# Feed-forward of a decoder layer by seven block products per pair of row tiles

## The chip, the cores and the metric

One core of a Trainium2 chip runs the whole kernel. The metric is the time of one execution in device microseconds, the median of several runs.

## The reference

The input x has 16 batches of 256 rows of 2048 numbers, 4096 rows in all. A layer does three things, each followed by a residual sum and a layer norm:

```python
x = _layernorm(x + _L0_attn_ref(x))              # autocorrelation along the row
x = _layernorm(x + _L0_xattn_ref(ctx, ctx, x))   # attention of 256 rows over 256 context rows
x = _layernorm(x + _L0_ffn_ref(x, W_base, gate_W, A, B))
# the last one, on rows xf of 2048 numbers:
gate_probs = softmax(xf @ gate_W.T)              # 8 experts
weights, sel = top_k(gate_probs, 2); weights = weights / sum(weights)
h = einsum('td,erd->ter', xf, A) * (w_dense[:, :, None] * 2.0)   # 8 experts x rank 8
out = xf @ W_base.T + einsum('ter,eor->to', h, B)                # W_base is 2048 x 2048
```

The change concerns the third of them, the feed-forward: a product with a 2048 x 2048 matrix, a router that picks two of eight experts for each row, and a LoRA term from a stack of 64 numbers per row.

## The kernel before, in words

`decoder_layer` runs `setup`, `attention_pass` (the first two things of the layer, on 16 batches), reads a verdict flag, and runs a slow exact autocorrelation only if a row needs it; with these inputs none does. Then `feed_forward` follows. `attention_pass` leaves its result x2 in HBM (`x_scratch` in the profile). At its end its SP queue already loads what the feed-forward starts with: the first 128 rows (`xn0`), the router and A matrices (`ag_raw`), and three chunks of W_base.

`feed_forward` works on 32 tiles of 128 rows. Every f32 operand is split in a high and a low f16 part, and a product is three matmuls: high x high, high x low of the weights, low of the rows x high. For a tile, `main(j)` runs 16 steps of 128 in the contraction x 3 terms for each of four blocks of 512 columns, in PSUM bank `ps_y[j]` (line 1143): 192 matmuls. `experts` computes the router scores and the A part in 16 pairs of narrow matmuls (lines 1162 and 1163) with 144 and 72 columns. `transposed_h` (line 1170) turns the weighted h by two TensorE transposes, and `lora(j)` adds two matmuls to each bank (lines 1147, 1148). The weights are loaded once as 32 chunks of two steps x 512 columns, scaled and split (ScalarE line 938 the high part, VectorE line 1012 the low one, and every fourth from the eighth on by GpSimd in lines 920 and 921). They stay in SBUF.

The row operands: SP loads a tile of x2 (`load`, line 875), ScalarE writes the high half of all 2048 numbers (line 949), VectorE the low one (line 1029), and SP issues two DMA transposes (lines 896 and 898) to `x_hi` and `x_lo`, double-buffered by tile; the first two tiles are turned by TensorE instead (line 1128). A bank is emptied by `bank_out(j)` on VectorE (line 1023): PSUM x inverse scale + the residual row, into `y`. Then come statistics (line 1039) and aggregation (line 1111) on VectorE, four small operations on GpSimd (lines 926 to 929), normalising on ScalarE (line 999) and the store by SP (line 901). TensorE waits in `main(j)` only until bank j of the tile before is empty. TensorE, VectorE, ScalarE and GpSimd run this over the middle tiles in a loop of two tiles a turn. Each engine executes its list in the written order, and semaphores tie the lists.

## Time and profile before

| | us |
|---|---|
| median of 3 runs | 2074.72 (2074.20 to 2074.81) |
| the profiled execution | 2074.21 |
| its span, first to last instruction | 2072.4 |

The profile is one execution. Its page has the busy time of each engine (PE is TensorE's matmuls, PEld its weight loads, DVE is VectorE, ACT ScalarE, POOL GpSimd, SP the queue that issues the DMAs), the chain of work that ended last, and groups of instructions by line. The attention fills roughly the first 590 us and the feed-forward the rest. A matmul's busy time is longer than the distance to the next one, since matmuls are pipelined: for what one costs, read the distance between starts. PEclk is the clock granted to TensorE as a share of 2.4 GHz; 0.50 is 1.2 GHz. The DMA share is the mean busy share of the core's 16 DMA engines.

### The profile page before, as it was taken

The page shows a single profiled execution, that of the slowest core. Times are in us where ns is not written, and L with a number is a line of the kernel's source. Part 1 is how long each engine was busy: PE and PEld are TensorE (multiplying, and loading weights), DVE is VectorE, ACT ScalarE, POOL GpSimd, SP SyncE. Part 2 cuts the span into 40 slices and gives each one's busy share as a digit, 9 for nine tenths or more (in the row PEclk, how much of TensorE's full clock was granted, in tenths as well). Part 3 has the DMA queues.
Part 4 walks back from the last instruction along what each step waited for, and adds up shares of the span by engine and source line. Part 5 has one row for each costly group of instructions (what it writes and reads, how often), then busy time and mean ns, then how long its engine had stood idle before and what let it go on. Part 6 is the DMA issues. An engine that isn't in the chain of part 4 may idle for free.

```text
span 2072.4 us, 28247 instructions
## 1 busy us (share of the span) xinstructions
PE 1952.7 (94%) x11266; PEld 1046.0 (50%) x11266; DVE 855.5 (41%) x2169; ACT 607.0 (29%) x771; POOL 318.3 (15%) x527
## 2 busy tenths in 40 slices
PE   3898989898957999999999999999999999999998
PEld 3666666666623444444444444444444444444443
DVE  4777777787757332222232222232222223222221
ACT  5777777778546110000010000010000011000000
POOL 3344444444315000000000000000000000000000
PEclk9999999999979999999999999999999999999999
DMA  8899999999667232121232111222111122211121
GB/s 265 231 281 260 291 269 282 266 288 272 203 211 249 85 93 66 61 61 61 71 100 71 61 61 61 61 97 85 61 61 61 61 81 92 70 61 61 61 61 41
DMA packets 288910, 271.17 MB, mean 131 GB/s; under 512 B 261504, under 2 KB 261632, under 8 KB 265984
## 3 DMA queue, kind: packets, MB, share of 16 engines
q1 hardware_dynamic: 288832, 270.17, 43.6%
q8 instruction: 44, 0.72, 0.1%
q14 instruction: 34, 0.28, 0.0%
HBM read 138.02 MB, written 67.11 MB: 99 GB/s over the span
## 4 chain that ended last, share of the span: by engine, by line
PE 67%; ACT 1%; DVE 1%; DMA 1%; issue 1%; POOL 1%; ACTq 0%; POOLq 0%
PE ps_y_f L1143 62%; PE ps_a_f L1162 2%; PE ps_y_f L1147 1%; PE ps_y_f L1148 1%; PE ps_a_f L1163 1%; ACT w_hi_f L938 1%; DMA cbuf<-w_chunks 0%; DVE w_lo_f L1012 0%; DMA chunk<-w_chunks 0%; POOL w_lo_f L921 0%; POOL cbuf L920 0%; PE ps_h_f L1170 0%; DVE b_stack_f L1098 0%; ACT y_f L999 0%; PE ps_t_f L1128 0%
## 5 line engine op out<-in xcount | busy, mean ns | idle before, releaser
L1143 PE MATMUL ps_y_f<-w_hi_f,x_hi_f 128*128 128x512 f16 x2048 | 777.5, 380 | 11.8 <-POOL w_lo_f L921 8.1
L1143 PE MATMUL ps_y_f<-w_lo_f,x_hi_f 128*128 128x512 f16 x2048 | 777.4, 380 | 0.0
L1143 PE MATMUL ps_y_f<-w_hi_f,x_lo_f 128*128 128x512 f16 x2048 | 777.2, 379 | 0.0
L999 ACT ACTIVATE y_f<-y_f,nb_f,rs_f 128x2048 f32<-128x2048 f32 x32 | 67.0, 2093 | 1112.3 <-POOL nb_f L929 1112.3
L1143 PEld LDWEIGHTS ps_y_f<-w_hi_f,x_hi_f 128*128 128x128 f16 x2048 | 200.6, 98 | 249.5 <-POOL w_lo_f L921 10.5
L1143 PEld LDWEIGHTS ps_y_f<-w_hi_f,x_lo_f 128*128 128x128 f16 x2048 | 200.7, 98 | 242.5 <-issue 1.4
L1143 PEld LDWEIGHTS ps_y_f<-w_lo_f,x_hi_f 128*128 128x128 f16 x2048 | 200.7, 98 | 233.5 <-issue 1.1
L1023 DVE SCALAR_TENSOR_TENSOR y_f<-ps_y_f,w_iscale,xn_f 128x512 f32<-128x512 f32 x64 | 46.6, 749 | 476.5 <-PE ps_y_f L1148 476.5
L1023 DVE SCALAR_TENSOR_TENSOR y_f<-ps_y_f,w_iscale,xn 128x512 f32<-128x512 f32 x64 | 46.6, 748 | 448.4 <-PE ps_y_f L1148 448.4
L926 POOL TENSOR_TENSOR var_eps_f<-mv_f,columns 128x1 f32<-128x1 f32 x32 | 6.1, 190 | 1357.1 <-DVE mv_f L1111 1357.1
L675 PE MATMUL ps_s_fast<-k_both_fast,q_hi_fast 128*128 128x256 f16 x1024 | 170.1, 274 | 6.2 <-DMA k_both_fast<-v_lo_fast 5.3
L675 PE MATMUL ps_s_fast<-k_both_fast,q_lo_fast 128*128 128x256 f16 x512 | 140.3, 274 | 0.0
L534 DVE SCALAR_TENSOR_TENSOR x2buf_fast<-ps_c_fast,iscale_fast,xbuf_fast 128x512 f32<-128x512 f32 x128 | 96.0, 750 | 70.3 <-PE ps_c_fast L664 69.5
L675 PEld LDWEIGHTS ps_s_fast<-k_both_fast,q_hi_fast 128*128 128x128 f16 x1024 | 100.6, 98 | 21.7 <-DMA k_both_fast<-v_lo_fast 5.5
L505 DVE TENSOR_TENSOR q_lo_fast<-ps_t_fast,q_hi_fast 128x512 f16<-128x512 f32 x128 | 86.2, 685 | 48.1 <-ACT q_hi_fast L389 48.0
L664 PE MATMUL ps_c_fast<-v_hi_fast,p_hi_fast 128*128 128x512 f16 x256 | 97.0, 379 | 0.1
L664 PE MATMUL ps_c_fast<-v_hi_fast,p_lo_fast 128*128 128x512 f16 x256 | 97.0, 379 | 0.0
L664 PE MATMUL ps_c_fast<-v_lo_fast,p_hi_fast 128*128 128x512 f16 x256 | 97.0, 379 | 0.0
L646 PE MATMUL ps_t_fast<-ident,xbuf_fast 128*128 128x128 f32 x512 | 75.0, 281 | 14.4 <-ACT xbuf_fast L422 9.0
L1039 DVE BATCH_NORM_STATS2 stats_f<-y_f 128x6 f32<-128x512 f32 x128 | 85.3, 687 | 2.2
L714 PE MATMUL ps_t_fast<-ag_raw,fwd_fast 128*128 128x256 bf16 x512 | 61.1, 273 | 25.9 <-ACT power_fast L465 25.9
L646 PEld LDWEIGHTS ps_t_fast<-ident,xbuf_fast 128*128 128x128 f32 x512 | 62.2, 145 | 37.6 <-DVE q_lo_fast L505 12.9
(161 smaller groups left out, 2081.4 us busy)
## 6 DMA issues: line engine op xcount, KB each, us to landing
xbuf_fast<-x SPq DMA_DIRECT2D x32, 1024.0 KB, 7.7
x_scratch<-x2buf_fast SPq DMA_DIRECT2D x32, 1024.0 KB, 6.0
out<-y_f SPq DMA_DIRECT2D x32, 1024.0 KB, 4.0
cbuf<-ctx_in SPq DMA_DIRECT2D x16, 1024.0 KB, 5.7
cbuf_fast<-ctx_in SPq DMA_DIRECT2D x16, 1024.0 KB, 6.8
xn<-w_chunks SPq DMA_DIRECT2D x16, 1024.0 KB, 7.6
xn<-x_scratch SPq DMA_DIRECT2D x16, 1024.0 KB, 4.8
xn_f<-x_scratch SPq DMA_DIRECT2D x16, 1024.0 KB, 4.8
```

Of the source, the lines that this page charges most:

```text
L505: v.tensor_tensor(q_lo[at], bank, q_hi[at], ALU.subtract).then_inc(t_free, 1)
L534: v.scalar_tensor_tensor(x2buf[parity][:, r, b * BANK:(b + 1) * BANK], ps_c[j % 2][:], iscale[parity][:], xbuf[parity][:, r, b * BANK:(b + ...
L646: ins = nc.tensor.transpose(bank[:, i * P:(i + 1) * P], xbuf[other][:, r, (kk + i) * P:(kk + i + 1) * P], ident[:])
L664: ins = nc.tensor.matmul(ps_c[j % 2][:], pp[:, d, r * P:(r + 1) * P], vv[parity][:, d, b * BANK:(b + 1) * BANK], start=(i == 0), stop=(i = ...
L675: ins = nc.tensor.matmul(ps_s[r][:, 0:C], qq[:, k, r * P:(r + 1) * P], k_both[other][:, k, part, :], start=(i == 0), stop=(i == 3 * KT - 1))
L714: ins = nc.tensor.matmul(ps_t[m % 3][:, 0:C], fwd[:, k, m * P:(m + 1) * P], u_t[:, k, :], start=(k == 0), stop=(k == HALF // P - 1))
L938: nc.scalar.activation(w_hi[chunk_at(c)], chunk[buffer_of[c]], ACT.Copy, scale=w_scale[:]).then_inc(w_hi_done, 1)
L999: nc.scalar.activation(y[parity][:], y[parity][:], ACT.Identity, bias=nb_[:, 0:1], scale=rs[:, 0:1]).then_inc(out_ready, 1)
L1023: v.scalar_tensor_tensor(y[parity][:, at], ps_y[j][:], w_iscale[:], xn[parity][:, at], ALU.mult, ALU.add).then_inc(evacuated, 1)
L1039: return v.bn_stats(stats[:, j], y[parity][:, j * BANK:(j + 1) * BANK])
L1143: nc.tensor.matmul(ps_y[j][:], xx[parity][:, k], ww[:, k, j * BANK:(j + 1) * BANK], start=(k == 0 and xx is x_hi and ww is w_hi), stop=False)
L1162: nc.tensor.matmul(ps_a[:, 0:2 * AG], x_hi[parity][:, k], ag_t[:, k, :], start=(k == 0), stop=False)
```

## The change

The feed-forward is rewritten; of the attention only the prefetch at its end changes (one load of 1 MB for the first weight unit in place of three of 0.5 MB). No arithmetic of the attention changes.

Rows are taken in 16 pairs of tiles, and output columns in two passes of 1024. For a pair and a pass, the operand rows are a 2 x 2 grid of blocks of 128 rows x 1024 numbers (A11, A12 the first tile's halves, A21, A22 the second's), the weights a 2 x 2 grid of 1024 x 512, and the output a 2 x 2 grid of 128 x 512. The four output blocks are built from seven products of sums of blocks in place of eight products. There are 32 slots: 0 to 15 are the pairs in order for the first 1024 columns, 16 to 31 the pairs in reverse order for the others; slot 16 uses the operands of slot 15 again. The lists of all engines are written out, without loops.

- The seven row operands of a slot: two plain blocks and five sums (`combine`, VectorE, 128 x 1024 f32), each split in a high half (`high_rows`, ScalarE) and a low half (`low_rows`, VectorE) and turned by one DMA transpose of 128 x 2048 f16 (`turn`, SP). `rows` has two buffers, `a_cols` one place per product. Operand i of slot s + 1 is turned when product i of slot s is done.
- The seven weight operands: for each of eight steps of a pass, `unit_low` makes five sums and differences in four VectorE instructions (1024, 512, 512 and 512 columns) and three low parts (1024, 1536 and 1024), `unit_high` three high parts on ScalarE. GpSimd takes no part. The second pass's weights overwrite the first's during slots 15 and 16.
- The seven products use seven PSUM banks. `update` adds a bank, times plus or minus the inverse scale, to a block of y: 14 updates of 128 x 512 a slot. y begins as the residual, loaded by SP from x2.
- The first pass's y goes to HBM (`y_scratch`) and comes back in the second pass for the statistics and the norm. The h of the router goes through `h_scratch`.
- The router of a pair works on both tiles at once (`router_scores`, `router_weights`), its scores run a pair ahead from slot 1 on, as narrow matmuls on four of the seven operands. Slots 0, 15 and 16 (`sweeps`) have the step as the outer loop over all seven products; the others finish one product after the other.

The core of the diff:

```diff
-                for c in range(PREFETCHED):
-                    sp.dma_start(consts["chunks"][c].rearrange("p k c -> p (k c)"), chunk_rows(w_chunks, c)).then_inc(prefetched, 16)
+                sp.dma_start(consts["cbuf0"][:], w_chunks[0]).then_inc(prefetched, 16)
...
+    OPERANDS = [(A22,), (A11,), (A21, A11, ALU.subtract), (A21, A22, ALU.add), (A12, A22, ALU.subtract), (A11, A22, ALU.add),
+                (A11, A12, ALU.add)]
+    W_SLOT = [1, 0, 2, 5, 3, 4, 6]
+    SCORED = (0, 1, 2, 4)
+    PRODUCT = {0: [(0, C11, 1), (0, C21, 1)], 1: [(1, C12, 1), (1, C22, 1)], 3: [(3, C21, 1), (3, C22, -1)],
+               5: [(5, C11, 1), (5, C22, 1)], 6: [(6, C12, 1), (6, C11, -1)], "L12": [("L12", C12, 1)],
+               "L21": [("L21", C21, 1)], "L22": [("L22", C22, 1)], "L11": [("L11", C11, 1)]}
...
+                def next_block(s, b):
+
+                    if s > 1 and makes(s) and s != NP_ + 1:
+                        if b in (A11, A12):
+                            sp.wait_ge(a_sum, 5 * made(s))
+                        else:
+                            sp.wait_ge(a_lo, item(s, 0) - NM + (4 if b == A21 else 6))
+                        load_block(s, b)
+
+                def turn(s, i):
+
+                    if makes(s):
+                        g = item(s, i)
+                        sp.wait_ge(a_lo, g + 1)
+                        if s:
+                            sp.wait_ge(pe_done, ev(s - 1, "S1" if s - 1 == 1 and i in SCORED else i))
+                        sp.dma_start_transpose(a_cols[:, i], rows[g % 2][:].rearrange("p a c -> p (a c)")).then_inc(a_turned[g % 2], 16)
...
+                    if s == NP_:
+                        sp.wait_ge(w_lo_done, 3 * (2 * HK - 1))
+                        for b in (A22, A21):
+                            load_block(s + 1, b)
+                        sp.wait_ge(w_lo_done, 3 * 2 * HK)
+                        for b in (A11, A12):
+                            load_block(s + 1, b)
+                        load_first(s)
+                    turn(s + 1, 0)
+                    turn(s + 1, 1)
+                    if s > NP_:
+                        store_out(s - 1)
+                    turn(s + 1, 2)
+                    if s > NP_:
+                        load_first(s)
+                    turn(s + 1, 3)
+                    next_block(s + 2, A21)
+                    load_residual(s + 1)
+                    turn(s + 1, 4)
+                    if s < LAST:
+                        store_h(s)
+                    turn(s + 1, 5)
+                    for b in (A22, A11, A12):
+                        next_block(s + 2, b)
+                    load_h(s + 1)
+                    turn(s + 1, 6)
...
+                    v.tensor_tensor(both[:, 0:2], raw[:, 0::2], raw[:, 1::2], ALU.add).then_inc(w_sum, 1)
+                    v.tensor_tensor(both[:, 2], raw[:, 0], raw[:, 3], ALU.add).then_inc(w_sum, 1)
+                    dve.wait_ge(w_sum, 4 * u + 1)
+                    v.tensor_tensor(raw[:, 1], raw[:, 1], raw[:, 3], ALU.subtract).then_inc(w_sum, 1)
+                    v.tensor_tensor(raw[:, 2], raw[:, 2], raw[:, 0], ALU.subtract).then_inc(w_sum, 1)
+                    low(slice(5, 7), raw[:, 0::3], 1)
+                    low(slice(2, 5), both, 2)
+                    low(slice(0, 2), raw[:, 1:3], 3)
...
+                def update(s, *which):
+
+                    for u in which:
+                        origin, (t, j), sign = updates(s)[u]
+                        acc = y[s % 2][:, t, j * BANK:(j + 1) * BANK]
+                        so_far = [w for w in range(u) if updates(s)[w][1] == (t, j)]
+                        if so_far:
+                            dve.wait_ge(added, NU * s + so_far[-1] + 1)
+                        else:
+                            dve.wait_ge(residual, 16 * (s + 1))
+                        dve.wait_ge(pe_done, ev(s, origin))
+                        v.scalar_tensor_tensor(acc, bank[bank_of(s, origin)][:], (w_iscale if sign > 0 else minus_iscale)[:], acc, ALU.mult,
+                                               ALU.add).then_inc(added, 1)
...
+                    low_rows(s + 1, 0)
+                    if 1 < s < LAST:
+                        router_scores(s)
+                    combine(s + 1, 2)
+                    low_rows(s + 1, 1)
+                    if 1 < s < LAST:
+                        router_weights(s)
+                    update(s, 0, 1)
+                    low_rows(s + 1, 2)
+                    combine(s + 1, 3)
+                    update(s, 2, 3)
+                    combine(s + 1, 4)
+                    low_rows(s + 1, 3)
+                    update(s, 4, 5)
+                    low_rows(s + 1, 4)
+                    combine(s + 1, 5)
+                    if late(s):
+                        router_scores(s)
+                    else:
+                        update(s, 6, 7, 8, 9)
+                    combine(s + 1, 6)
+                    low_rows(s + 1, 5)
+                    if late(s):
+                        router_weights(s)
+                        update(s, 6, 7)
+                    else:
+                        update(s, 10, 11)
+                    low_rows(s + 1, 6)
+                    if late(s):
+                        update(s, 8, 9)
+                    if s > NP_:
+                        block_stats(s, C21)
+                        block_stats(s, C22)
+                        first_stats(s)
...
+                def step(i, kk):
+
+                    for part, ww in ((0, w_hi), (0, w_lo), (HK, w_hi)):
+                        ins = nc.tensor.matmul(bank[i][:], a_cols[:, i, part + kk, :], ww[:, W_SLOT[i], kk, :],
+                                               start=(kk == 0 and part == 0 and ww is w_hi), stop=(kk == HK - 1 and part == HK and i not in (2, 4)))
+                    return ins
+
+                def product(s, i):
+
+                    wait_slot(s, i)
+                    wait_bank(s, i)
+                    for kk in range(HK):
+                        ins = step(i, kk)
+                    done(ins, s, i)
...
+                def sweep(s):
+
+                    for kk in range(HK):
+                        if s != LAST:
+                            pe.wait_ge(w_lo_done, 3 * (HK * (s // NP_) + kk + 1))
+                        for i in range(NM):
+                            if kk == 0:
+                                wait_slot(s, i)
+                                wait_bank(s, i)
+                            ins = step(i, kk)
+                            if kk == HK - 1:
+                                done(ins, s, i)
+                                if i == 2:
+                                    lora(s, "L22")
+                                if i == 4:
+                                    lora(s, "L11")
...
```

## Rows read from the trace of the kernel before

**Rows 1.** Page, part 1: busy us (share of the span) and instructions.

```profile
PE 1952.7 (94%) x11266; PEld 1046.0 (50%) x11266; DVE 855.5 (41%) x2169; ACT 607.0 (29%) x771; POOL 318.3 (15%) x527
```

**Rows 2.** Page, part 4: the chain that ended last, by engine.

```profile
PE 67%; ACT 1%; DVE 1%; DMA 1%; issue 1%; POOL 1%; ACTq 0%; POOLq 0%
```

**Rows 3.** Windows: the attention, steady tiles; first line names the columns.

```profile
core 0: us, PE busy (x) PEld busy (x) DVE busy (x) ACT busy (x) POOL busy (x), PEclk, DMA share, GB/s
0.00:560.00 560.00, 483.20 (x3568) 345.52 (x3569) 415.28 (x959) 406.86 (x579) 247.60 (x370) 0.99 0.93 267
1000.00:1500.00 500.00, 500.00 (x2609) 236.51 (x2608) 130.67 (x385) 50.45 (x45) 11.84 (x44) 1.00 0.23 70
```

**Rows 4.** Timeline of SP: start, duration us, line; first transposes of two tiles.

```profile
1040.06 1.52 SPq L896 DMA_TRANSPOSE x_hi_f<-cbuf  x1
...
1084.95 1.67 SPq L896 DMA_TRANSPOSE x_hi_f<-cbuf  x1
```

**Rows 5.** Chain in order of time, from 590 us: start, us, what.

```profile
686.06 10.36 PE ps_y_f L1143 x48
```

**Rows 6.** Timeline, router scores in a steady tile.

```profile
1077.15 0.20 PE L1163 MATMUL ps_a_f<-ag_t_f,x_lo_f 128*128 128x72 f16 x1
...
1077.24 0.20 PE L1163 MATMUL ps_a_f<-ag_t_f,x_lo_f 128*128 128x72 f16 x1
```

**Rows 7.** Timeline, where the feed-forward begins, ScalarE and TensorE.

```profile
599.24 1.06 ACT L966 ACTIVATE y_f<-ag_raw 128x1024 f32<-128x1024 f32 x1 [9.48 <-issue]
...
612.25 0.63 PE L1143 MATMUL ps_y_f<-w_hi_f,x_lo_f 128*128 128x512 f16 x1
612.67 0.63 PE L1143 MATMUL ps_y_f<-w_hi_f,x_hi_f 128*128 128x512 f16 x1
```

**Rows 8.** Windows of the start, columns as in Rows 3.

```profile
613.00:615.00 2.00, 2.00 (x6) 0.76 (x5) 2.00 (x2) 2.00 (x4) 0.00 (x0) 0.50 0.39 96
617.00:619.00 2.00, 2.00 (x10) 0.87 (x9) 2.00 (x2) 2.00 (x3) 0.00 (x0) 0.94 0.77 227
639.00:641.00 2.00, 0.34 (x2) 0.00 (x0) 2.00 (x2) 0.05 (x1) 2.00 (x1) 1.00 0.97 406
```

**Rows 9.** Groups of VectorE by shape: busy us, mean ns, idle before.

```profile
L505 DVE TENSOR_TENSOR q_lo_fast<-ps_t_fast,q_hi_fast 128x512 f16<-128x512 f32 x128 | 86.2, 685 | 48.1 <-ACT q_hi_fast L389 48.0
...
L1029 DVE TENSOR_TENSOR cbuf<-xn,cbuf 128x2048 f16<-128x2048 f32 x15 | 34.3, 2285 | 0.2 <-ACT cbuf L949 0.2
...
L1079 DVE TENSOR_SCALAR dense_f<-expert_ids,top_f_f,wtop_f 128x8 f32<-128x8 f32 x32 | 9.3, 291 | 1.2
```

**Rows 10.** Timeline of VectorE: two weight low parts, two bank updates, two statistics.

```profile
615.56 2.48 DVE L1012 SCALAR_TENSOR_TENSOR w_lo_f<-y_f,w_scale,w_hi_f 128x1024 f16<-128x1024 f32 x2
...
1055.27 1.41 DVE L1023 SCALAR_TENSOR_TENSOR y_f<-ps_y_f,w_iscale,xn_f 128x512 f32<-128x512 f32 x2 [11.90 <-PE ps_y_f L1148]
1056.60 1.28 DVE L1039 BATCH_NORM_STATS2 stats_f<-y_f 128x6 f32<-128x512 f32 x2
```

**Rows 11.** Groups of ScalarE by shape.

```profile
L999 ACT ACTIVATE y_f<-y_f,nb_f,rs_f 128x2048 f32<-128x2048 f32 x32 | 67.0, 2093 | 1112.3 <-POOL nb_f L929 1112.3
...
L938 ACT ACTIVATE w_hi_f<-cbuf,w_scale 128x1024 f16<-128x1024 f32 x12 | 13.6, 1144 | 7.6 <-DMA cbuf<-w_chunks 7.5
```

**Rows 12.** Page, part 6: DMA issues, median us to landing.

```profile
x_hi_f<-cbuf SPq DMA_TRANSPOSE x30, 3.8
```

**Rows 13.** The attention's transposes to k_both, issued by SP.

```profile
DMA to landing us min/median/max: 4.2/4.8/12.6
```

**Rows 14.** Windows: two transposes alone, plain loads; columns as in Rows 3.

```profile
1041.00:1047.00 6.00, 6.00 (x31) 2.78 (x30) 2.37 (x2) 0.39 (x1) 0.00 (x0) 1.00 0.77 175
631.00:633.00 2.00, 2.00 (x11) 0.89 (x10) 1.74 (x12) 1.22 (x2) 0.00 (x0) 1.00 1.03 422
```

**Rows 15.** Timeline of the end: last matmul and last store.

```profile
2062.43 0.38 PE L1148 MATMUL ps_y_f<-b_stack_f,ag_raw 128*128 128x512 f16 x1
...
2068.09 0.33 SPq L901 DMA_DIRECT2D out<-y_f  x1
```

951 lines of the change are left out of this document (582 added, 369 removed).

## The prediction

> **What bounds the kernel now.** I read the totals first, then the chain, then stages. TensorE is busy 94% of the span, VectorE 41%, ScalarE 29% [rows 1], and 67% of the chain that ended last is TensorE [rows 2]. The windows say where: between 1000 and 1500 us TensorE is busy all 500 us at full clock, while VectorE has 131 us, ScalarE 50 and the DMA engines a share of 0.23 [rows 3]. So in the feed-forward only TensorE's own instructions count. From one row transpose to that of the next tile are 44.89 us [rows 4]. 48 main matmuls take 10.36 us, 0.216 each [rows 5]; a pair of router matmuls takes 0.095 [rows 6]. 200 wide ones (192 main, 8 LoRA) make 43.2 us, 16 router pairs 1.5, two transposes 0.1: 44.8, the tile. The sum closes, no wait is hidden in it. The block begins its work at 599.2 and its first matmuls run 0.42 us apart [rows 7]. The attention before it is only touched in its prefetch.
>
> **The change, part by part.** *Matmuls.* A pair of tiles now takes 384 main matmuls. With seven products of two halves it takes 2 passes x 7 products x 8 steps x 3 terms = 336. LoRA stays at 16 a pair. Router matmuls stay too: four operands x 8 steps x a hi/lo pair = 32 pairs against 2 x 16. A first-pass slot (pair of tiles, half of the columns) is 176 x 0.216 = 38.0, plus 32 x 0.095 = 3.0, plus four transposes 0.2: 41.2 us. A second-pass slot is 38.0. Together 79.2 against 89.8, so 10.6 less a pair and 169 us over 16 pairs, if TensorE stays the bound.
>
> *VectorE.* No row adds two f32 tensors in SBUF. The nearest are subtractions: 2048 columns 2.28 us, 512 columns 0.69 [rows 9]. That is 1.04 ns a column, so 1024 columns are 1.2 us, and some 1.14 from start to start, because successive starts lie about 0.08 closer than the durations (two of 1.28 each end within 2.48 [rows 10]). The bounds are half of that, were such an addition to run at double rate, and 1.2. I take 1.14. A slot has 5 sums and 7 low halves (12 x 1.14 = 13.7) and 14 bank updates of 0.66 (two in 1.41 [rows 10]) = 9.2. The router of two tiles is some 29 small operations, none over 0.29 [rows 9]; I take 6, at most 8.4. That makes 29 of 41.2 us in the first pass. In the second, eight statistics at 0.6 [rows 10] and the aggregation replace the router: 28.5 of 38.0. VectorE is in order and waits in between for TensorE, but each product's operand is made a slot ahead and a bank is reused six products later, so a lag under some 10 us reaches nobody.
>
> *ScalarE.* 7 high halves of 1.1 [rows 11], and in the second pass four normalising halves of about 1.05: 12 of 38 us. Hidden.
>
> *Transposes.* 217 of them in place of 60, all from SP, each with 2 KB a partition as before. One lands after 3.8 us [rows 12], next to the attention's traffic typically 4.8 and at most 12.6 [rows 13]. Two row buffers alternate, so two items take one round: landing 3.8, high half 1.1, low half 1.2, handovers: some 7 us, 25 a slot. SP also waits for product i before it overwrites operand i. Queued behind that wait are the block loads of a later pair, the residual and the stores; each has between 5 and 30 us until it is needed.
>
> *DMA engines.* Two transposes alone held a share of 0.77 over 6 us, 2.3 us each; a plain stream ran at 422 GB/s [rows 14], so 1 MB is 2.5 us. A second-pass slot moves 7 transposes (16.2 us) and 6.3 million bytes (2 MB of x, 1 residual, 1 of first-half result in, 2 out: 15 us) = 31 of 38. But in the attention the mix got 267 GB/s at a share of 0.93 [rows 3]; at that price the 10 million bytes of such a slot take 35 us. The first-pass slot moves 4.3 plus 3.7 million: 26 to 28 of 41. I count both as hidden. Without the cover see the first rival.
>
> *The start.* TensorE now needs all seven operands for its first step, and VectorE makes the weight sums. One unit (1/8 of a half): one 1024-wide sum 1.14, three of 512 at 0.61, low parts 1.20 + 1.75 + 1.20: 7.1 us, against 21 x 0.216 = 4.5 of TensorE. From 599.2, VectorE's list (four units, seven low halves, five sums, scale steps) ends at 643; the seventh transpose lands by 648. Until then TensorE idles for the most part at half clock; two cold steps cost 3 us more (before, the clock rose about 6 us after the first matmuls [rows 7, 8]). Router scores are done at 664, and VectorE, waiting for them, goes on with units 6 and 7 and the weights until 685. The last step ends at 690. The next slot waits for the bank that only the last updates free (13 x 0.66 and five other operations after 685): 698. It has two pairs' scores: 45.4, to 743. Thirteen slots of 41.2: 1279.
>
> *The turn of the passes.* Slots 15 and 16 walk the steps outermost while eight new units are made. VectorE: end of the last slot and router 7, bias stack 1, eight units 57, 15 updates 10, hence the last unit at 79 after the turn; TensorE ends 4.5 + 1 later, 84.5. Slot 17's operands come after that: blocks of x wait for the stage buffer, then 2 MB go ahead of the first transpose, so products 0 to 2 run late by 4 us. VectorE's backlog (13 updates, 12 sums and halves) delays slot 18's first bank by 5. I get 169 us for slots 15 to 18 where 152 would be undisturbed: 1448. Thirteen more of 38.0: 1942.
>
> *The end.* Before, from the last matmul to the end were 10.0 us [rows 15]. Now two updates, two statistics and four shorter ScalarE operations with two stores follow: 13.5. Sum: 1955. The profiled execution took 2074.2 with a span of 2072.4; with those 1.8 us around it the forecast is 1957. The median of the runs, 2074.7, is 0.5 above it.
>
> **A rule on the clock.** Between two steps of the paced slots TensorE would wait 2.6 us. In the old start it was busy 0.34 of 2 us at 639 and still had the full clock [rows 8]. The Trainium skill (TensorE: Matmul & The Clock Gate, HAM oscillation) says that a step shorter than its wait falls back to the low clock each time. By the trace the sum above stands; by that rule ten steps take 9 us in place of VectorE's 7.1.
>
> **Rivals.** *DMA binds the second pass.* For: at the attention's rate the slot needs 35 of 38 us, and SP issues in order with waits between, so the engines can't be filled. Against: each 1 MB has about 5 us of spread, and 422 GB/s was reached. Were a slot 40.5 to 43, 15 slots add 38 to 75: 1995 to 2032.
>
> *VectorE's order binds.* Its 75% are counted without semaphore times; 2 us a slot over 29 slots: 2015; 1 us: 1986. Against: the slack of 10 us at each bank.
>
> *The low clock in the paced steps.* By the rows of cold matmuls, 0.42 apart [rows 7], a step of 21 takes 9 us; ten steps 19 us more: 1976. Against it stands the window at 639.
>
> *Slower than before: the transpose round.* If transposes in the new, denser traffic land late, the two row buffers set the slot: 7 items x (landing + 2.9)/2. From a landing of about 8 us this exceeds a second-pass slot; from about 9.5 us, 43.4 a slot, the gain of all is gone, and at the longest landing seen, 12.6 [rows 13], a slot is 54 us and the kernel takes about 2370. For: 3.6 times the transposes and more plain bytes beside them. Against: typical landings in the attention at a share of 0.93 were 4.8.
>
> *It doesn't do what it says.* All streams are now written out; if TensorE's longer stream ran short of instructions, each of 5400 matmuls at 0.25 instead of 0.216 would eat the gain. Against: the attention, written out too, kept TensorE busy 483 of 560 us with shorter instructions [rows 3].
>
> **How the numbers follow.** Forecast as worked: 0.62, 1942 to 1972 (VectorE's additions at double rate would give some 25 us back at start and turn; small waits add). DMA-bound second pass 0.17. VectorE's order 0.09. Low clock 0.05. Transposes' round 0.04, split between little gain and a loss. Not as said 0.03. The forecast is 1957. The range of 8 in 10 takes in the forecast's, the clock's, most of VectorE's and a good half of the DMA's case: 1938 to 2020. A measurement here can tell about 0.2%, 4 us, from no change. Faster 0.94, same 0.01, slower 0.05.
>
> **What would show it.** Right: main matmuls 5376; in 800 to 1200 and 1500 to 1900 us TensorE busy throughout, VectorE at 0.70 to 0.75; slots 41.2 and 38.0 apart; first full step at about 650; slot 1 starting near 698; steps 7.1 apart near 1330 to 1360 with the clock at 1.00. Wrong: TensorE waiting for transposes in the second pass with landings over 6 us and a DMA share near 0.9 (first rival), waits for updates on VectorE in mid-slot (second), 0.50 in the clock column at the turn (third).

## The result, and the profile after

| | before | after |
|---|---|---|
| median, us | 2074.76 (4 runs, 2074.20 to 2078.83) | 2016.6 (4 runs, 2013.05 to 2023.17) |
| the profiled execution | 2074.21 | 2013.05 |
| its span | 2072.4 | 2011.1 |

The ratio of the times is 0.9719, with a 95% interval of 0.9691 to 0.9747. The kernel is 58 us faster; the forecast was a gain of 118 us. The direction was right and 2016.6 lies in the range, near its end, but the gain is only half of what the forecast 1957 promised.

Page of the changed kernel, part 1 (busy us, share of the span, instructions) and the lines of part 2 that show the stages:

```profile
PE 1801.7 (90%) x10466; PEld 968.3 (48%) x10466; DVE 1459.2 (73%) x2673; ACT 799.4 (40%) x984; POOL 308.7 (15%) x449
...
PE   3899989999862879999999999997799999999997
...
PEclk9999999999985989999999999999899999999998
DMA  8899999999859497888888787736999999999994
```

TensorE's busy time fell by about the work removed, its share from 94% to 90% [rows 1]. VectorE went from 41% to 73%. In the last line the DMA engines, at 0.23 in the middle of the old feed-forward [rows 3], are at 7 or 8 tenths in the first pass and at 9 in the second until its last slice.

A slot is read from the start of its first main matmul (line 1486) to that of the next slot. The terms of the forecast stand against these lengths, in us of the profiled execution:

| stretch | forecast | measured | miss |
|---|---|---|---|
| start, until slot 1 begins | 698 | 698.6 | +0.6 |
| slot 1 | 45.4 | 63.8 | +18.4 |
| slots 2 to 14 | 13 x 41.2 | 13 x 41.25 | +0.7 |
| slots 15 to 18 | 169 | 38.3 + 51.1 + 56.1 + 38.0 = 183.5 | +14.5 |
| slots 19 to 31 | 13 x 38.0 = 494 | 514.6, 39.6 each on average (38.0 to 43.9) | +20.6 |
| end | 13.5 | 14.4 | +0.9 |

The misses add to 55.7; 2011.1 - 1955 is 56.1, and the difference is rounding. Three places hold 53.5 of it. Windows of the steady parts (columns as in [rows 3]): slots 4 to 14, slots 19 to 31, and slots 19 to 30 alone, since in slot 31 no further operands are made:

```profile
845.50:1298.60 453.10, 453.10 (x2681) 224.98 (x2680) 320.84 (x660) 90.92 (x110) 0.00 (x0) 1.00 0.81 192
1482.10:1996.70 514.60, 498.89 (x2289) 223.54 (x2287) 362.71 (x479) 148.54 (x137) 45.64 (x52) 0.99 0.98 247
1482.10:1958.60 476.50, 460.79 (x2114) 206.45 (x2113) 339.95 (x444) 142.09 (x132) 44.41 (x48) 0.99 1.01 254
```

In the first pass TensorE has no gap at all (453.10 of 453.10), VectorE 0.71. In the second, TensorE stands 15.7 of 514.6 us. Slots 19 to 30 are 39.7 us each, and the DMA share in them is 1.01 where I had counted "31 of 38" to "35 of 38". The waits of the same stretch (engine, line, what it waited for: us in all, times, longest):

```profile
ACT rows_f L1114 <- DMA a_cols_f<-rows_f: 242.0, 48, 8.3
DVE rows_f L1233 <- ACT rows_f L1114: 140.4, 47, 6.8
...
PE bank_f L1524 <- DVE y_f L1272: 15.7, 10, 4.3
```

Read from below: TensorE's LoRA matmuls (line 1524) wait for an update of VectorE (line 1272), and VectorE, in order, stands before that update at a low half (line 1233) whose high half is not there. In all, ScalarE is late with high halves mostly because a row buffer is still read by a transpose (242.0 us), but right before TensorE's waits there is one link more. The longest of them ends at 1593.4. VectorE and ScalarE before it:

```profile
1571.91 1.23 DVE L1233 TENSOR_TENSOR rows_f<-sums_f,rows_f 128x1024 f16<-128x1024 f32 x1 [6.79 <-ACT rows_f L1114]
...
1589.63 1.23 DVE L1233 TENSOR_TENSOR rows_f<-sums_f,rows_f 128x1024 f16<-128x1024 f32 x1 [5.15 <-ACT rows_f L1114]
```

```profile
1570.82 1.06 ACT L1114 ACTIVATE rows_f<-sums_f 128x1024 f16<-128x1024 f32 x1 [8.34 <-DMA a_cols_f<-rows_f]
...
1584.02 1.24 ACT L1154 ACTIVATE cbuf<-cbuf,nb_f,rs_f 128x1024 f32<-128x1024 f32 x1 [2.11 <-POOL nb_f L1096]
...
1588.56 1.04 ACT L1114 ACTIVATE rows_f<-sums_f 128x1024 f16<-128x1024 f32 x1
```

A late transpose holds ScalarE for 8.34 us and VectorE behind it for 6.79. Its statistics come late by that, then GpSimd's four operations, then ScalarE's four normalising halves (lines 1154 and 1155). They stand in ScalarE's list ahead of the high half that VectorE needs at 1589.6. The same normalising halves stand before each of the seven waits of over 1 us in slots 19 to 30. So the name at TensorE is VectorE's, the far end of the chain is a DMA, and between them lies the order of ScalarE's list. The transposes themselves (SP's instruction in ns, then landing), first pass and second:

```profile
L947 SPq DMA_TRANSPOSE a_cols_f<-rows_f x77: 1317/1960/4992, 844.4 to 1292.2; - x77
...
DMA to landing us min/median/max: 4.2/4.6/7.4
```

```profile
L947 SPq DMA_TRANSPOSE a_cols_f<-rows_f x87: 1317/3398/7962, 1479.8 to 1968.2; - x87
...
DMA to landing us min/median/max: 4.2/6.0/10.2
```

A landing of 3.8 [rows 12] was assumed. No transpose here lands in under 4.2, and the median of the second pass is 6.0. Slot 1 has a wait of another kind (waits from 699 to 765):

```profile
PE bank_f L1515 <- DVE ag_raw L1339: 13.5, 1, 13.5
PE bank_f L1486 <- DVE y_f L1272: 6.9, 1, 6.9
PE bank_f L1524 <- ACT ag_raw L1148: 1.5, 1, 1.5
```

The 6.9 end at 698.6 and belong to the forecast's start (its "698"). The 13.5 are new: the transposed h of slot 1 waits for the last operation of the router on VectorE, and 1.5 more for ScalarE's copy of it. After each of the two long waits TensorE runs at the low clock: 0.50 from 698 to 702 and again from 746 to 758.

### The profile page after: what moved, and what is told of

It reads as the page before. It is cut to its first block and busy times, and to the rows that moved or that the text cites. A ratio compares the mean times of both kernels' runs of the same rounds, so it can differ in the third digit from the quotient of the medians.

```text
span 2011.1 us, 27872 instructions
## 1 busy us (share of the span) xinstructions
PE 1801.7 (90%) x10466; PEld 968.3 (48%) x10466; DVE 1459.2 (73%) x2673; ACT 799.4 (40%) x984; POOL 308.7 (15%) x449
## 5 line engine op out<-in xcount | busy, mean ns | idle before, releaser
L1486 PE MATMUL bank_f<-w_hi_f,a_cols_f 128*128 128x512 f16 x3584 | 1093.1, 382 | 75.8 <-DMA a_cols_f<-rows_f 60.0
L1486 PE MATMUL bank_f<-w_lo_f,a_cols_f 128*128 128x512 f16 x1792 | 685.4, 382 | 0.0
L1486 PEld LDWEIGHTS bank_f<-w_hi_f,a_cols_f 128*128 128x128 f16 x3584 | 353.1, 99 | 506.8 <-DVE w_lo_f L1241 41.8
L1272 DVE SCALAR_TENSOR_TENSOR y_f<-bank_f,w_iscale,y_f 128x512 f32<-128x512 f32 x384 | 269.4, 743 | 137.2 <-PE bank_f L1486 98.0
L1486 PEld LDWEIGHTS bank_f<-w_lo_f,a_cols_f 128*128 128x128 f16 x1792 | 176.4, 98 | 205.5 <-issue 5.2
L1114 ACT ACTIVATE rows_f<-xn_f 128x1024 f16<-128x1024 f32 x93 | 98.2, 1056 | 380.1 <-DMA xn_f<-x_scratch 152.0
L1233 DVE TENSOR_TENSOR rows_f<-sums_f,rows_f 128x1024 f16<-128x1024 f32 x93 | 113.6, 1221 | 166.5 <-ACT rows_f L1114 166.3
L1114 ACT ACTIVATE rows_f<-sums_f 128x1024 f16<-128x1024 f32 x93 | 97.9, 1052 | 324.7 <-DMA a_cols_f<-rows_f 317.2
L1233 DVE TENSOR_TENSOR rows_f<-xn_f,rows_f 128x1024 f16<-128x1024 f32 x93 | 112.7, 1212 | 24.7 <-ACT rows_f L1114 24.4
L339 POOL TENSOR_TENSOR u_rows_fast<-xbuf_fast 128x1024 bf16<-128x1024 f32 x32 | 75.7, 2366 | 33.4 <-DMA xbuf_fast<-x 26.8
```

The source lines that it names most:

```text
L339: g.tensor_tensor(u_rows[:, r], xbuf[parity][:, r, 0:HALF], xbuf[parity][:, r, HALF:L], ALU.subtract).then_inc(folded, 1)
L1114: nc.scalar.activation(rows[g % 2][:, 0], source(i), ACT.Copy).then_inc(a_hi, 1)
L1233: v.tensor_tensor(rows[g % 2][:, 1], source(i), rows[g % 2][:, 0], ALU.subtract).then_inc(a_lo, 1)
L1272: v.scalar_tensor_tensor(acc, bank[bank_of(s, origin)][:], (w_iscale if sign > 0 else minus_iscale)[:], acc, ALU.mult, ALU.add).then_inc(a ...
L1486: ins = nc.tensor.matmul(bank[i][:], a_cols[:, i, part + kk, :], ww[:, W_SLOT[i], kk, :], start=(kk == 0 and part == 0 and ww is w_hi), st ...
```

## The experiments

Four questions: what makes a slot of the second pass 39.6 us and not 38.0; what makes slot 1 63.8 and not 45.4; what the turn of the passes loses; and whether the answers give a faster kernel. Slot lengths are those of one execution each. The changed kernel itself spreads over 10 us between executions, so whole times serve here only for differences beyond that, the lengths of slots for the rest. As a measure of what slot lengths mean: with the second pass unchanged, slots 19 to 30 average 39.7 us in the changed kernel, 39.9 with the scores ahead in slot 1, and 40.0 with stores added in the first pass.

### Slot 1: the scores before the products

In the changed kernel slot 1 gives its event `S1` only after the scores of operand 4, which stand behind five products, and the transposes of slot 2 wait for that event. The forecast had not seen this wait. The edit puts each operand's scores ahead of its product, so that a transpose waits for its own product only:

```diff
-            return [0, 1, 2, 3, 4, "S1", 5, 6, "L22", "L11", "L12", "L21", "S2"]
+            return [0, 1, 2, 3, "S1", 4, 5, 6, "L22", "L11", "L12", "L21", "S2"]
-                            sp.wait_ge(pe_done, ev(s - 1, "S1" if s - 1 == 1 and i in SCORED else i))
+                            sp.wait_ge(pe_done, ev(s - 1, i))
...
-                        product(s, i)
-                        if late(s):
-                            if i in SCORED:
-                                ins = scores(s, i)
+                        if late(s) and i in SCORED:
+                            ins = scores(s, i)
                             if i == 4:
                                 done(ins, s, "S1")
-                        else:
+                        product(s, i)
+                        if not late(s):
```

> Slot 1 takes 63.8 us in the changed kernel, 18 more than counted. In slot 1 the transposes of operands 0, 1, 2 and 4 of slot 2 wait until all router scores of slot 1 are done, 31 us into the slot; VectorE reaches the router of slot 1 only behind the low half of operand 5. Here each operand's scores are computed before its product, and a transpose waits for its own product alone. Theory (the wait for the scores holds the row work back and with it the router): slot 1 falls to 46 to 50 us, TensorE's wait before the transposes of h (13.5 us) goes to under 2, the kernel gets 14 to 18 us faster. Rival (the transposes' own round of issue, landing, high and low half sets the slot, whatever releases it): slot 1 stays above 56 us. The slots from 2 on stay as they are.

Measured: 2008.35 us; slot 1 58.6 in place of 63.8. The event cost 5.2 us, not 14 to 18, and 58.6 lies where the rival put it. What is left (waits from 697 to 760):

```profile
PE bank_f L1515 <- DVE ag_raw L1339: 10.8, 1, 10.8
PE bank_f L1524 <- ACT ag_raw L1148: 0.7, 1, 0.7
```

### The second pass: order on SP, bytes, or VectorE

Three edits. The first moves the stores, the load of the first half, the residual and three of four x blocks to GpSimd's queue from slot 17 on. The second loads 128 of the 1024 columns of each first half, 0.9 MB less a slot:

```diff
-                    sp.dma_start(y_first, y_scratch[token(s)]).then_inc(first_loaded, 16)
+                    sp.dma_start(y_first[:, :, 0:P], y_scratch[token(s)][:, :, 0:P]).then_inc(first_loaded, 16)
```

The third leaves out VectorE's four statistics of the first half from slot 17 on.

> From slot 17 on the stores of the result, the loads of the first half, of the residual and of three of the four blocks of x are issued by GpSimd instead of SP; the bytes are the same, and A21 and h stay on SP. Second-pass slots 19 to 31 take 39.6 us on average in the changed kernel against 38.0 of TensorE's work. Theory A (order: in one queue a transpose stands behind 1 to 2 MB of plain transfers, lands after 6 to 9 us in place of 4.3, and the row work and VectorE's updates get late): slots 38.0 to 38.4, transposes land in 4 to 5.5 us. Theory B (capacity: the DMA engines at a share of 0.98 can carry no more): slots stay at 39.2 or more whichever queue issues. Theory C (VectorE's own time): no change either.

> The load of the first half's result in the second pass brings 128 of 1024 columns per row tile; the rest of that half of the output is computed from old contents of the buffer. That is 0.9 million bytes less of 10 in each second-pass slot, with all other work kept. Theories A (order) and B (capacity) both say that slots 19 to 31 fall from 39.6 to 38.0 to 38.6 us; by B the DMA share stays near 0.95. Theory C (VectorE's own time) says 39.6 as before.

> The four statistics instructions on the first half are left out from slot 17 on, so the norm there uses old statistics; VectorE has 2.45 us less in each second-pass slot, all DMAs stay. Theory C (VectorE's own time binds the second pass): slots 19 to 31 fall from 39.6 to 38.0 to 38.3 us. Theories A and B: VectorE stands idle for ScalarE's halves anyway, slots fall by at most 0.6 us.

Measured: 2076.21, 1994.42 and 2025.66 us. Without 0.9 MB every slot from 18 to 30 is 37.99 us and TensorE has no wait left, although transposes still land after a median of 5.1 us and up to 10.2. Without the statistics (2.5 us less for VectorE a slot) slots 19 to 30 average 40.7, no better than 39.7; TensorE waited 23.5 us for updates. So bytes count, and less work for VectorE gained nothing. With the plain transfers on GpSimd's queue slots 19 to 30 rose to 44.5. That one left two readings: an expensive issuer, or a second queue of any kind. Windows of slots 19 to 30 with 0.9 MB less, and of the second pass with GpSimd's queue:

```profile
1484.00:1939.90 455.90, 455.90 (x2114) 206.67 (x2113) 343.38 (x449) 143.91 (x133) 44.52 (x48) 1.00 0.98 244
```

```profile
1490.00:2016.00 526.00, 470.51 (x2093) 206.84 (x2092) 334.05 (x437) 139.38 (x131) 67.72 (x132) 0.96 1.00 227
```

At a share of 0.98 of 37.99 us, 37.2 us of the engines, nothing waits; at 1.01 it does.

### Added stores in the first pass

```diff
+                def spill_out(s, n):
+                    if 3 <= s <= 13 and n < (2 if s <= 8 else 4):
+                        sp.dma_start(spill[spills[0]], consts["cbuf0"][:]).then_inc(spilled, 16)
+                        spills[0] += 1
...
+                    spill_out(s, 1)
                     turn(s + 1, 3)
...
                     turn(s + 1, 4)
+                    spill_out(s, 0)
...
+                    spill_out(s, 2)
                     turn(s + 1, 6)
+                    spill_out(s, 3)
```

> The second pass of the changed kernel moves some 10 MB a slot (2 MB more than the first) at a DMA share of 0.99 and takes 39.6 us a slot where TensorE needs 38.0; leaving 0.9 MB out gave 38.0. Two theories are left. Capacity: the engines are simply full, at (0.99 x 39.6 - 0.79 x 41.25) / 2 = 3.3 us for each further MB. Order: what counts is that transposes stand behind plain transfers on SP's queue and land at 6 to 10 us instead of 4.3, however full the engines are. This kernel adds stores of 1 MB each from an idle buffer to a spare DRAM area in the first pass: two in each of slots 3 to 8 (10 MB a slot, as in the second pass), four in each of slots 9 to 13 (12 MB). Capacity: slots 3 to 8 need 32.6 + 6.6 = 39.2 us of the engines, under TensorE's 41.25, and stay at 41.25 each without a wait of TensorE; slots 9 to 13 need 32.6 + 13.2 = 45.8 and take 45 to 47 at a share of 0.99 or more; the kernel takes about 2040. Order: already slots 3 to 8 show landings of 6 to 10 us, waits of TensorE and 42 to 44 us a slot.

Measured: 2027.06 us. Windows of slots 3 to 8, 9 to 11 and 12 to 14:

```profile
804.30:1051.80 247.50, 247.50 (x1469) 122.91 (x1466) 175.28 (x361) 49.59 (x60) 0.00 (x0) 1.00 0.95 246
1051.80:1175.50 123.70, 123.70 (x735) 61.37 (x732) 85.75 (x179) 24.80 (x30) 0.00 (x0) 1.00 0.99 266
1175.50:1308.10 132.60, 124.81 (x737) 60.99 (x735) 87.19 (x181) 24.91 (x31) 0.00 (x0) 1.00 1.00 263
```

With the bytes of a second-pass slot, slots 3 to 8 are 41.25 us each and TensorE never waits; the engines are busy 0.95 x 41.25 = 39.2 us of them, as expected to the tenth. Transposes land there after a median of 4.8 us and 8.2 at most, where the theory of order wanted 6 to 10. Two stores cost (0.95 - 0.81) x 41.25 = 5.8, so 2.9 us for each MB. Four stores were expected to bind at once; in fact slots 9 to 11 still took 41.25, and only 12 to 14 stretched to 45.2, 43.8 and 43.6. In slots 9 to 11 the engines moved 266 GB/s, 11.0 million bytes a slot of the 12.1 asked for, so the rest fell behind into the slots after. The theory of order falls as the main cause: 10 MB with plain transfers at similar places of SP's list do no harm where the slot is 41.25, and cost 1.6 to 1.7 where it is 38.0. The engines' capacity decides, at 39.2 us for this mix; the 0.5 us from there to 39.7 no run explains.

### Plain copies for the transposes

```diff
-                        sp.dma_start_transpose(a_cols[:, i], rows[g % 2][:].rearrange("p a c -> p (a c)")).then_inc(a_turned[g % 2], 16)
+                        sp.dma_start(a_cols[:, i].rearrange("p k c -> p (k c)"), rows[g % 2][:].rearrange("p a c -> p (a c)")).then_inc(a_turned[g % 2], 16)
```

> Every transpose of the feed-forward is replaced by a plain copy of the same 0.5 MB between the same two buffers, so the columns of x are not transposed and all main products, the router's scores and the whole output are other values; the number of instructions and of waits stays. If the transposes are what fills the engines (7 of them at some 2.9 us, 20 of 39 us, against 1.3 for plain data at the 2.5 us a MB of an undisturbed stream, 9 us), the DMA share of the first pass falls from 0.79 to about 0.5 and that of the second from 0.99 to about 0.7, landings are 3 us or less, all slots of the second pass take 38.0, slot 17 falls below 50, and the kernel takes 1975 to 1990. If copies within SBUF cost the engines as much as transposes, the shares stay and so do the 39.6 us.

Measured: 1986.51 us. First and second pass:

```profile
850.00:1290.00 440.00, 440.00 (x2608) 218.61 (x2607) 309.90 (x634) 88.73 (x106) 0.00 (x0) 1.00 0.51 190
1490.00:1950.00 460.00, 460.00 (x2133) 208.49 (x2131) 340.71 (x446) 145.60 (x134) 45.74 (x50) 1.00 0.72 266
```

The bytes are the same, the share falls from 0.81 to 0.51 and from 1.01 to 0.72, and all slots from 18 on are 37.99. Per transpose that is (0.81 - 0.51) x 41.25 / 7 = 1.8 us more than a plain copy in the first pass, and (1.01 x 39.7 - 0.72 x 38.0) / 7 = 1.8 in the second. The whole second-pass slot of 10 MB takes 0.72 x 38.0 = 27.4 us when all of it is plain, 2.7 us a MB, so a plain 0.5 MB is about 1.4 and a transpose some 3.2. The packet records of the changed kernel give 2.9 to 3.0 directly: the transposes' packets of 256 bytes take 20.6 us of the engines in a first-pass slot and 20.9 in a second-pass one. The Trainium skill (Advanced Engine Details and Errata, X-Bar Transpose (TRN2)) states that "TRN2 transpose DMAs are as fast as regular DMAs"; by these runs, for 0.5 MB within SBUF, one takes more than twice as long. Slot 17 stayed at 53.2 and slot 1 at 60.9, each 2.9 us shorter: neither is mainly a matter of what a transpose costs.

### Orders alone: router of slot 1, updates of the second pass

```diff
+                    if s > NP_:
+                        update(s, 0, 1)
                     low_rows(s + 1, 1)
...
+                    if late(s):
+                        router_scores(s)
+                    if s > NP_:
+                        update(s, 2, 3)
                     low_rows(s + 1, 2)
                     combine(s + 1, 3)
+                    if late(s):
+                        router_weights(s)
```

(ScalarE's exponential and its copy of h move ahead accordingly; the scores stand ahead of the products, as above.)

> Orders alone. (1) Slot 1, on top of scores before products: VectorE's router scores and weights of slot 1 stand right behind the event of the scores (in place of after the sum of operand 5 and the low half of operand 5), ScalarE's exponential and the copy of h stand ahead of the high halves 2 and 5. In the run with the scores ahead alone, TensorE still waited 10.8 us for the router's last operation and 0.7 for the copy; if that is all that is left, slot 1 falls from 58.6 to 46 to 48 us. If the transposes bind slot 1 instead, it stays over 54. (2) Second pass: the updates of product 0 and of product 1 stand ahead of the low halves 1 and 2 of the next slot. TensorE waits 15.7 us in all there for updates that the LoRA products need, each time with VectorE held by a low half that waits for a late transpose. If VectorE's order turns late transposes into TensorE's waits, these waits go and the slots fall from 39.6 to 38.0 to 38.3. If the DMA engines' capacity binds, the waits only move to the transposes (TensorE waiting for a_cols) and the mean stays at 39.3 to 39.9. Whole: 1980 to 1985 with the first, about 1997 with the second.

Measured: 2029.94 us. Both halves went against the wish. Slot 1 is 61.2 although the router's wait is gone; other waits stand in its place (from 702 to 765, without the one that ends where slot 1 begins):

```profile
PE bank_f L1510 <- DMA a_cols_f<-rows_f: 6.6, 1, 6.6
PE bank_f L1491 <- DVE y_f L1270: 4.2, 1, 4.2
PE bank_f L1529 <- ACT ag_raw L1148: 2.7, 1, 2.7
```

In the second pass the LoRA matmuls no longer wait, and the slots rise to 40.9: TensorE now waits 27.5 us, 11 times, at a slot's first product for the bank that the last updates of the slot before free. My reading, not tested by itself: VectorE standing at an update that TensorE has not made ready delays the next operand, which keeps a row buffer longer. At a full share (1.00 in slots 19 to 30) this order moved the wait and lost about 1 us a slot. An order that moves ScalarE's normalising halves behind the high halves that VectorE needs, the link seen in the profile above, was not run.

### Stores and one load on ScalarE's queue

> The two stores of the result and the load of the first half move from SP's queue to ScalarE's in the second pass (3 MB of the 6.5 MB of plain data), with the same bytes; in the earlier run with plain transfers on GpSimd's queue the slots rose to 44. If SP's order is the limit (plain transfers ahead of transposes in one ring), transposes land in 4.3 to 6 us more often and the second pass falls to 38.0 to 38.5 a slot, the kernel to 1995 to 2000. If the engines' capacity is the limit, the slots stay at 39.3 to 40 and the kernel at 2008 to 2017; if a second queue mixes its packets between those of a transpose and slows it, they rise above 40.5.

Measured: 2070.15 us, the third case: slots 19 to 30 average 43.8. Window of slots 19 to 30 and, below it, the transposes of the second pass:

```profile
1490.40:2016.00 525.60, 473.80 (x2112) 209.17 (x2113) 340.11 (x445) 143.46 (x133) 40.27 (x48) 0.95 1.02 231
```

```profile
L947 SPq DMA_TRANSPOSE a_cols_f<-rows_f x85: 1667/3527/14579, 1488.4 to 2014.1; - x85
...
DMA to landing us min/median/max: 4.2/7.2/19.8
```

At a full share the engines move 231 GB/s in place of 254, and a transpose lands after up to 19.8 us. GpSimd's queue had given 227. So it is not the one issuer that costs: plain data from a second queue beside transposes makes them dearer. By the packet records the transposes of a slot take 24.3 us of the engines in both runs where they took 20.9, and the plain data 19.6 and 19.2 where it took 18.6. The Trainium skill (DMA: Bandwidth & Descriptors, Rules for kernel authors) states that spreading DMAs over queues doesn't help, since all run on the same 16 engines. By these two runs it does harm: 4.1 and 4.8 us a slot.

### Three operands kept from the first pass

The first pass has room (0.81 of 41.25 us), the second has none, and a transpose costs more than twice what a plain transfer of its size does. So, with the scores ahead in slot 1 as well, operands 4, 5 and 6, once transposed, go to HBM in slots 1 to 14 and come back as plain loads in slots 17 to 30:

```diff
+                def keep(s, i):
+                    if 0 < s < LAST and i in KEPT:
+                        g = item(s, i)
+                        sp.wait_ge(a_turned[g % 2], 16 * (g // 2 + 1))
+                        sp.dma_start(a_scratch[s, KEPT.index(i)], a_cols[:, i].rearrange("p k c -> p (k c)")).then_inc(a_kept, 16)
...
+                    if kept(s, i):
+                        g = item(s, i)
+                        sp.wait_ge(a_lo, g + 1)
+                        sp.wait_ge(pe_done, ev(s - 1, i))
+                        sp.dma_start(a_cols[:, i].rearrange("p k c -> p (k c)"), a_scratch[token(s), KEPT.index(i)]
+                                     ).then_inc(a_turned[g % 2], 16)
+                        return
```

> The runs so far say: the second pass is bound by the DMA engines (10 MB a slot, 39.2 us of them); a transpose of 0.5 MB costs 3.0 us of them where a plain copy of the same size costs 1.3; the first pass has 8 us a slot to spare. This kernel (with the scores ahead in slot 1) uses that: operands 4, 5 and 6, transposed in the first pass, are stored to a DRAM area (slots 1 to 14) and loaded from there in the second pass (slots 17 to 30) where they were summed, split and transposed again; a placeholder of one column keeps the counts. Same result. First pass: 1.5 MB more, 32.6 + 5 = 37.6 us of the engines, so 41.25 a slot. Second pass: 3 x (3.0 - 1.6) = 4.1 us less, 35.1 us: slots 19 to 30 at 38.0 each, share near 0.92. VectorE also loses 3 sums and 3 low halves, 7 us a slot, which lets slots 17 and 18 end 3 to 8 us earlier. Whole 1980 to 1988. Rival (latency of a load behind plain data as bad as that of a transpose): slots stay at 39 or more and the kernel above 2000.

Measured: 1990.14 us. Windows of slots 4 to 14 and 19 to 30:

```profile
845.70:1299.50 453.80, 453.80 (x2690) 225.36 (x2688) 321.62 (x661) 90.93 (x110) 0.00 (x0) 1.00 0.90 230
1479.70:1935.50 455.80, 455.80 (x2113) 206.65 (x2112) 272.53 (x445) 115.18 (x133) 47.14 (x48) 1.00 0.93 268
```

Expected shares: 37.6 of 41.25 = 0.91, and 35.1 of 38.0 = 0.92. Both slots are as expected, 41.25 and 37.99, without a wait of TensorE. Slot 17 fell to 52.9, by 3.2. With the engines' load under the slot, the irregular part of the second pass is gone. VectorE has less to do here too (272.53 us for 339.95), so this run alone does not say which of the two did it; the run without statistics, where less of VectorE's work gained nothing, and the one with 0.9 MB less, where all of it stayed, say that it was the engines' load.

### What is left of slot 1, and the turn

The plain copies together with both reorderings of slot 1:

> What binds slot 1 (63.8 us in the changed kernel, 58.6 with the scores ahead). With the router's operations moved forward as well, TensorE's wait for them went (from 10.8 us to 2.7), but slot 1 took 61.2: it then waited 6.6 us for the transposed operand 4 of slot 2. From 691 to 759 us twelve transposes followed each other, 5.7 us each, behind block loads. Here every transpose is replaced by a plain copy of the same bytes (so main products, scores and the output are other values), with both reorderings of slot 1 kept. Theory: three layers, event, router, round of transposes; with the third taken away slot 1 is 46 to 49 us. Rival: something fourth (the block loads, VectorE's share) holds it above 54. The rest as with plain copies alone: second pass at 38.0; whole 1968 to 1975.

Measured: 1983.13 us, slot 1 53.7 and slot 2 42.5. It lies between what theory and rival said. TensorE still waited for operands (from 697 to 800, after the start of slot 1):

```profile
PE bank_f L1485 <- DMA a_cols_f<-rows_f: 4.9, 1, 4.9
PE bank_f L1504 <- DMA a_cols_f<-rows_f: 3.3, 1, 3.3
```

So what is left looks like the supply of operands as a whole (read from these waits, no run isolates it): a landing, a high half, a sum, a low half, each behind VectorE's list and the block loads, of which the transposes' own price is only a part (7.5 us: 61.2 against 53.7).

The kept operands with two orders at the turn: the load of h for slot 17 ahead of the block loads, and the updates of products 0 and 1 ahead of low halves 1 and 2 in slot 17 alone.

> As the kernel with three operands kept, and in addition two orders at the turn of the passes, where the changed kernel lost 14.5 us in slot 17: the load of h for slot 17 stands ahead of the block loads for slot 18 (TensorE waited 2.7 us for it), and in slot 17 VectorE's updates of products 0 and 1 stand ahead of the low halves 1 and 2 of slot 18 (TensorE waited 9.6 us for these updates, its clock falling to 0.50 and costing some 3 us more). If these two waits are what the slot loses, it falls by 12 us against the kernel without them, to 42 to 46; if, as in the run that moved the updates in all of the second pass, VectorE is only late by another road (low halves later, so slot 18's operands later), slots 17 and 18 together gain under 3 us.

Measured: 1985.45 us; slots 17 and 18 are 46.3 + 44.5 = 90.8 where they were 52.9 + 38.0 = 90.9. The second case: the wait moved from slot 17 to 18 and nothing was gained; the 4.7 us between the two runs lie ahead of them (slot 0 starts 0.7 earlier and takes 83.9 against 87.0, slot 16 50.5 against 51.1). The same kernel, timed:

> The kernel of the run before (scores ahead in slot 1, operands 4 to 6 kept from the first pass, two orders at the turn) timed against the kernel before, since single executions of the changed kernel spread from 2013 to 2023 and the comparison has to hold beyond that. The slots of the second pass were all 37.99 us, so the irregular part is gone; what is left to vary is the start (slot 0 was 83.9 to 87.0 us). Expected: 1984 to 1991 in every execution, a median of 1987, ratio to the kernel before 0.957, with an interval under 0.002 on either side; 30 us (1.5%) below the changed kernel. If the spread of the changed kernel came from elsewhere than the second pass, executions above 1995 will be among them.

Measured: 1989.06 us median of 5 (1986.15 to 1992.45), before 2075.49 of 9; ratio 0.9587, interval 0.9574 to 0.9600. The median is 2 us above what was expected, and one execution is above the 1991 that I gave as the most; none is above 1995. It is 27.5 us below the changed kernel's 2016.6.

## Why the prediction was right in direction and wrong in size

**Right.** *Matmuls:* slots of 41.25 in the first pass for 41.2, and 37.99 in the second wherever nothing waits for 38.0; the pipelined distance of 0.216 us [rows 5] carries over. *VectorE's durations:* an addition of two f32 tensors in SBUF is 1.22 us and successive ones start 1.13 to 1.14 apart, as taken from [rows 9, 10]; not the double rate. *VectorE's total* of 29 and 28.5 us a slot: 320.84 of 453.10 is 29.2 in a slot of 41.25, 339.95 of 476.50 is 28.3 in one of 39.7. *The start*: 698.6 for 698, and not by luck, since its stages agree: the first full step at 650.1 for 650, the last step's end at 691.7 for 690. *The last unit* came 78.2 after the turn for 79. *The end*: 14.4 for 13.5.

**Wrong, 20.6 us: "DMA engines ... I count both as hidden".** The forecast had both ends before it, 31 us from the rows of single streams [rows 14] and 35 from the attention's rate [rows 3], and both lay under 38. Measured it was 39.2: 0.95 of 41.25 in the run with the added stores, which has the transposes and the bytes of a second-pass slot without filling the engines. The term was mis-sized in two prices. A transpose was taken at 2.3 us, as two alone showed, and is 3.0 beside other traffic; plain data at 2.5 us a MB and is 2.7 to 2.9. Seven times 0.7 and 6.5 times 0.3 are 7 of the 8 us between 31 and 39.2. The attention's 267 GB/s, which I took as the pessimistic price, came from a mix with fewer transposes per byte: 33.6 of its 149 million bytes, against 3.7 of 10.1 here. The trace of before held the right prices, one level below the window that I read. The packets of the attention's 64 transposes take 190.4 us of the engines, 3.0 each, and its other 115 million bytes 327.5 us, 2.85 a million. By these a second-pass slot is 7 x 3.0 + 6.3 x 2.85 = 39.0, above 38.0. The rival "DMA binds the second pass" (0.17, slots of 40.5 to 43) named the mechanism. Of its signs the DMA share is there (1.01) and the landings half so (a median of 6.0); TensorE waiting for transposes is not, as its waits name VectorE. The measured 39.6 lies between the rival and the forecast.

**Wrong, 18.4 us: slot 1.** The forecast gave it 45.4, its matmuls alone; by the prediction's own terms, 38.0 + 2 x 3.0 + 0.2, they are 44.3. The trace has 14.9 us of waits in the slot, and the low clock after them and at its start takes most of the rest. The forecast passed over `turn`'s wait for `S1` (5.2 us, shown by the scores put first), over the place of the router in VectorE's list, behind the sum and low half that themselves wait (up to 13.5 us seen at TensorE), and over the supply of operands from slot 0 on. The last failed by the same term as above: the prediction's "some 7 us for two items, 25 a slot" was written for a landing of 3.8. In the run with the orders changed, twelve transposes followed each other from 691 to 759, 5.7 us each, 40 a slot. In the middle of a 41-us slot that is hidden, and behind slot 0, which frees all seven operands at once at its end, it is not. "A lag under some 10 us reaches nobody" does not hold for slots 1 and 17, where both the operands and the banks of the slot before come free only at its end. Nor is a bank always "reused six products later": the LoRA product for C21 takes bank 1 some 17 us after product 1 is done, and all ten waits of slots 19 to 30 stand there, so VectorE's lag was over 17 us each time.

**Wrong, 14.5 us: the turn.** Forecast for slots 15 to 18: 84.5 for the first two and 84.5 for the others; measured 38.3, 51.1, 56.1, 38.0. Slot 17 began 89.4 us after the turn for 84.5: the last unit was 0.7 early, the last step 2.2 longer (7.7 for 5.5, of it 1.9 by the clock, below), and TensorE then waited 3.4 for slot 17's first product. Slots 17 and 18 together are 94.1 for 84.5; slot 18 lost nothing. The waits of slot 17 (from 1388 to 1445; the 3.4 end where it begins) and two windows of it:

```profile
PE bank_f L1524 <- DVE y_f L1272: 9.6, 2, 5.6
PE bank_f L1486 <- DMA a_cols_f<-rows_f: 3.4, 1, 3.4
PE bank_f L1524 <- DMA ag_raw<-h_scratch: 2.7, 1, 2.7
```

```profile
1388.00:1392.00 4.00, 4.00 (x11) 1.51 (x12) 3.96 (x7) 1.06 (x1) 0.00 (x0) 0.57 0.49 91
...
1424.00:1428.00 4.00, 1.03 (x2) 0.13 (x2) 1.07 (x2) 2.94 (x3) 0.00 (x0) 0.50 1.10 298
```

The LoRA matmuls wait 12.4 us, and the low clock at the slot's start and after these waits takes most of the other 5.7 us above 38.0; the forecast had nothing for either, and of what it had, 4 us for products 0 to 2 and 5 for slot 18's first bank, neither is there. The longest wait, 5.6, is the same with plain copies and with kept operands, and in all three VectorE stands 2.9 us before the update for a high half that is behind ScalarE's four normalising halves. So part of what is left is an order on ScalarE; no run moved it. Kept operands took 3.2 of the 9.6 us, plain copies 2.9, and the two reorderings nothing; the rest stays open.

**The slower rival and the others.** "The transpose round" needed typical landings of 8 us; the median was 6.0, and the kernel was not slower. "VectorE's order binds, 1 to 2 us a slot" looks right in the waits of TensorE, all of which name VectorE, but it did not hold as a cause: with 2.5 us less work for VectorE nothing was gained, with another order some 1 us a slot was lost, and with less DMA work and VectorE's order as it was all waits went.

**The clock.** TensorE in the turn (start, us, idle time before it):

```profile
1362.12 0.39 PE L1486 MATMUL bank_f<-w_hi_f,a_cols_f 128*128 128x512 f16 x1 [1.93 <-DVE w_lo_f L1241]
...
1369.19 0.39 PE L1486 MATMUL bank_f<-w_hi_f,a_cols_f 128*128 128x512 f16 x1 [2.36 <-DVE w_lo_f L1241]
...
1376.91 0.39 PE L1486 MATMUL bank_f<-w_hi_f,a_cols_f 128*128 128x512 f16 x1 [3.02 <-DVE w_lo_f L1241]
```

```profile
1362.00:1366.00 4.00, 3.88 (x18) 1.78 (x19) 4.00 (x6) 2.16 (x2) 0.00 (x0) 1.00 0.70 178
...
1378.00:1382.00 4.00, 4.00 (x12) 1.51 (x11) 0.00 (x0) 0.00 (x0) 0.00 (x0) 0.59 0.84 280
```

In the turn three steps were paced by VectorE, after waits of 1.9, 2.4 and 3.0 us. The first two ran at the full clock, as the window of [rows 8] had suggested. After the third the granted clock was 0.59 over four us, and the last step with its three LoRA pairs took 7.7 us (1376.9 to 1384.6) where 27 matmuls at 0.216 are 5.8. So the forecast was right on two of three. The Trainium skill (TensorE: Matmul & The Clock Gate, HAM oscillation) describes steps that work for less time than they wait; here the steps work 4.5 us or more and wait at most 3.0, so its case did not occur, and the prediction's "by that rule" applied it to waits that it does not describe.

## What to carry to other kernels

Sum the DMA engines' time of a slot by kind of transfer, at prices from a stretch with the same mix, and treat a sum within 20% of the slot as a rival with a real chance: here 31 and 35 of 38 became 39.2, while the attention's own packets, taken by kind, give 39.0. A transpose of 0.5 MB within SBUF cost what 1.1 MB of plain data costs, so here keeping a transposed operand in HBM and loading it again beat making it twice, because the stretch that stores it had engine time to spare. When TensorE's waits name an engine that is at 70%, follow the chain to its end before reordering that engine's list.
